# The last group of attention: denominators summed on TensorE without transfers, reciprocals on VectorE, a split projection and four stores

## The chip, the cores and the metric

The kernel runs on one core of a Trainium2 chip. The metric is the device time of one execution in microseconds (us). Engines are named as the profile names them: PE is TensorE, DVE is VectorE, ACT is ScalarE, POOL is GpSimd, SP is SyncE, which here only issues transfers.

## The reference

The whole is a block of three layers over x of 2 x 2048 rows of 512 numbers, all float32:

```python
x = x + 0.5 * ffn(layernorm(x))      # mixture of 64 experts, top 6, plus a shared one
x = x + attn(layernorm(x))
x = x + 0.5 * ffn(layernorm(x))
```

The change is in the attention, in its last microseconds:

```python
q = (x @ Wq + bq).reshape(b, s, 16, 32).transpose(0, 2, 1, 3)   # 16 query heads of 32
k = x @ Wk + bk                                                 # one key head, one value head
v = x @ Wv + bv
attn = softmax(einsum('bhsd,btd->bhst', q, k) / sqrt(32))
out = einsum('bhst,btd->bhsd', attn, v).transpose(0, 2, 1, 3).reshape(b, s, 512)
return out @ Wo + bo
```

## The kernel before

Five stages follow one another, each closed by a barrier of all engines: route and experts (first ffn), attention, route and experts again, and a final addition. Attention takes 8 chunks (CHUNKS) of 512 queries (QT). A chunk has 4 groups (GPC) of 4 heads (HG), so there are 32 groups, numbered G from 0 to 31; group 31 is head group 3 of chunk 7. Each group walks over 16 steps (STEPS) of 128 keys:

- PE `scores` (L1397) writes the transposed scores of one head and 128 keys, 128 x 512, into one of three PSUM banks of `pS`. ACT (L1346) takes the exponential into `prob[step % 4]`, a tile for four heads. PE `values` (L1435) adds the product with v to `pO`, whose four blocks of 32 partitions are the four heads.
- The softmax denominators are sums of `prob` over all keys. POOL `add_pair` (L1301) adds the tiles of two neighbouring steps, in two halves of 128 x 1024; there are 8 such pairs in a group. Pairs 0 and 1 are written to `acc`; pairs 2 to 7 go to a ring of three `pair` tiles and are added to `acc` by an accumulating transfer of 1 MB that POOL issues (L1309). When three such transfers have landed on each `acc`, PE `denominators` (L1445) sums `acc` over the partitions with a matrix of ones into `pD`. For every group but 31 this is done in steps 4 and 5 of the next group.
- ACT `copy_d` (L1357) copies `pD` to SBUF. SP `reciprocals` (L1238 to L1249) writes the four rows to DRAM, reads them back spread over 128 partitions (`d_in`), DVE takes the reciprocal of 128 x 16 numbers (L1553), SP writes them to DRAM and reads them back repeated 32 times (`d_rec`, 128 x 512).
- DVE `copy_o` (L1549) takes `pO` out of PSUM, and POOL `normalise` (L1322) multiplies it with `d_rec` into `o_n[g]`.
- PE `output` (L1419) projects a chunk: for each of four tiles of 128 queries, four products, one for each head group, into a bank of `pM`. DVE `output` (L1527) adds the result to `xo`, and SP stores the chunk in one transfer of 1 MB (L1273 for the last chunk). For chunks 0 to 6 this is done within the next chunk.
- In all groups but 31, PE also computes the row maxima of the next group between the scores (`maxima`, L1410), which DVE reduces (L1522).

After the last step of group 31 nothing of the next group is there to fill the engines: denominators, reciprocals, normalisation, projection and store of chunk 7 follow one after another. The order of every engine's work is written out by hand; semaphores are the only links. The code that differs for the last group is static (outside the loops).

## Time and profile before

| | |
|---|---|
| three timed runs | 3488.95, 3485.11, 3488.79 us, median 3488.79 |
| profiled execution, its own time | 3486.42 us |
| its span | 3484.9 us |
| busy over the span: PE, DVE, ACT, POOL | 84%, 59%, 44%, 62% |
| attention's last group, steps 0 to 15 | about 2675 to 2719 us of the span |
| from the last `values` to the next stage's first instruction | 2719.4 to 2768.0 us |

All times are microseconds from the start of the span. A matmul of float32 is two instructions in the trace, so a product of 128 x 512 counts as x2. What matters here is the second half of the last group and the 49 us behind it, in which the rows of the section below lie.

### The profile page before, as it was taken

How to read it: one execution, taken by the hardware profiler on the slowest of the kernel's cores; microseconds unless marked ns; L12 is line 12 of the kernel's file. 1: busy time of each engine (PE TensorE's matmuls, PEld its weight loads, DVE VectorE, ACT ScalarE, POOL GpSimd, SP SyncE). 2: the span in 40 equal slices, each digit the busy share in tenths (PEclk: the TensorE clock that was granted, in tenths of full speed). 3: DMA queues.
4: the chain of work that ended last, by engine and by line, in shares of the span. 5: the costliest groups of instructions: out<-in, count | busy, mean ns of one | idle time of the engine just before them, and what ended most of it. 6: DMA issues, size and time to landing. Idle time of an engine off the chain costs nothing. (4 is left out here: it accounts for less than half of the span.)

```text
span 3484.9 us, 50220 instructions
## 1 busy us (share of the span) xinstructions
PE 2920.2 (84%) x15152; PEld 1575.4 (45%) x15152; DVE 2072.8 (59%) x3981; ACT 1525.6 (44%) x2837; POOL 2170.1 (62%) x1329
## 2 busy tenths in 40 slices
PE   7967677498999998999999989999999598667650
PEld 4644444254554444444444444444444255444430
DVE  7932223464877777777787767767775188222222
ACT  3422222142566565566565655655656243222220
POOL 2148887110588777687787876876878321678760
PEclk9988888698899999999999999999999799888885
DMA  6469999754466666666666665756666542899998
GB/s 215 178 181 240 238 243 217 224 202 142 80 139 139 130 152 126 144 139 129 153 131 133 150 129 132 149 109 145 137 125 136 147 151 103 218 238 237 230 188 289
DMA packets 218402, 582.86 MB, mean 167 GB/s; under 512 B 34448, under 2 KB 35472, under 8 KB 193424
## 3 DMA queue, kind: packets, MB, share of 16 engines
q0 software_dynamic: 84992, 343.98, 48.7%
q1 hardware_dynamic: 133136, 235.53, 20.7%
q8 instruction: 135, 2.21, 0.3%
q14 instruction: 139, 1.14, 0.1%
HBM read 231.23 MB, written 155.25 MB: 111 GB/s over the span
## 5 line engine op out<-in xcount | busy, mean ns | idle before, releaser
L1522 DVE TENSOR_REDUCE attention_mx<-attention_pM 128x1 f32<-128x512 f32 x2048 | 1272.5, 684 | 354.3 <-PE attention_pM L1410 333.4
L1346 ACT ACTIVATE attention_prob<-attention_pS 128x512 f32<-128x512 f32 x2048 | 1064.2, 603 | 642.4 <-PE attention_pS L1397 621.9
L1301 POOL TENSOR_TENSOR attention_pair<-attention_prob 128x1024 f32<-128x1024 f32 x384 | 928.6, 2504 | 196.8 <-ACT attention_prob L1346 196.6
L1397 PE MATMUL attention_pS<-attention_qT,attention_kT 128*128 128x512 f32 x2048 | 867.8, 429 | 48.4 <-issue 22.0
L1410 PE MATMUL attention_pM<-attention_kT,attention_qT 96*128 96x512 f32 x2048 | 837.0, 417 | 19.3 <-DMA attention_qT<-q_parts 10.3
L1397 PEld LDWEIGHTS attention_pS<-attention_qT,attention_kT 128*128 128x128 f32 x2048 | 387.4, 191 | 541.9 <-ACT attention_prob L1346 336.2
L1435 PE MATMUL attention_pO<-attention_prob,attention_v 128*32 128x512 f32 x4096 | 541.6, 606 | 0.0
L625 POOL DMA_INDIRECT sum<-experts_res,c_table x256 | 403.8, 1577 | 117.1 <-issue 81.8
L1410 PEld LDWEIGHTS attention_pM<-attention_kT,attention_qT 96*128 96x128 f32 x2048 | 396.1, 195 | 121.6 <-DVE attention_mx L1522 53.0
L1301 POOL TENSOR_TENSOR attention_acc<-attention_prob 128x1024 f32<-128x1024 f32 x128 | 307.4, 2472 | 178.9 <-ACT attention_prob L1346 178.7
L654 PE MATMUL experts_pT<-c_ident,experts_rows 128*128 128x128 f32 x1024 | 208.7, 371 | 242.1 <-DMA experts_rows<-xn_rows,c_table 235.8
L732 DVE COPY experts_xT<-experts_pT 128x512 f32<-128x512 f32 x128 | 88.5, 692 | 534.7 <-PE experts_pT L654 532.9
L609 POOL DMA_INDIRECT experts_rows<-xn_rows,c_table x256 | 249.5, 974 | 102.3 <-issue 71.3
L654 PEld LDWEIGHTS experts_pT<-c_ident,experts_rows 128*128 128x128 f32 x1024 | 168.4, 215 | 291.9 <-DMA experts_rows<-xn_rows,c_table 261.9
L1309 POOL DMA_DIRECT2D attention_acc<-attention_pair x192 | 169.4, 882 | 128.9 <-POOL attention_pair L1301 121.7
L668 PE MATMUL experts_pU<-experts_xT,experts_wup 128*64 128x256 f32 x2048 | 236.9, 384 | 2.0 <-DVE experts_xT L732 2.0
L699 ACT ACTIVATE experts_xT<-experts_pT 128x512 f32<-128x512 f32 x128 | 76.4, 597 | 359.5 <-PE experts_pT L654 359.5
L668 PEld LDWEIGHTS experts_pU<-experts_xT,experts_wup 128*64 128x64 f32 x2048 | 142.9, 138 | 115.1 <-issue 51.4
L267 POOL TENSOR_TENSOR route_eqp<-route_eq,route_count 128x1536 f32<-128x1536 bf16 x16 | 52.5, 3279 | 212.7 <-ACT route_count L373 212.7
L1435 PEld LDWEIGHTS attention_pO<-attention_prob,attention_v 128*32 128x32 f32 x4096 | 83.7, 108 | 200.9 <-issue 127.2
L681 PE MATMUL experts_pD<-experts_wdn,experts_hid 64*128 64x512 f32 x512 | 145.6, 692 | 3.7 <-DVE experts_hid L740 2.8
L713 ACT ACTIVATE experts_res<-experts_pD,experts_rows 128x512 f32<-128x512 f32 x128 | 87.8, 687 | 111.7 <-PE experts_pD L681 93.5
(125 smaller groups left out, 2408.9 us busy)
## 6 DMA issues: line engine op xcount, KB each, us to landing
attention_acc<-attention_pair POOLq DMA_DIRECT2D x192, 1024.0 KB, 7.8
experts_wup<-in_L_ffn_w_up_dram SPq DMA_DIRECT2D x128, 256.0 KB, 4.8
attention_qT<-q_parts SPq DMA_DIRECT2D x96, 256.0 KB, 7.2
xn_rows<-route_xn SPq DMA_DIRECT2D x16, 1152.0 KB, 6.0
sum<-route_sh SPq DMA_DIRECT2D x16, 1024.0 KB, 4.4
experts_wdn<-in_L_ffn_w_down_dram SPq DMA_DIRECT2D x64, 256.0 KB, 5.0
attentionp_got<-sum SPq DMA_DIRECT2D x16, 1024.0 KB, 8.9
combine_got<-sum SPq DMA_DIRECT2D x16, 1024.0 KB, 8.2
```

The source lines that it names most:

```text
L609: pool.indirect_dma_start(rows[e % RING][:, a * HALVES + h, :], None, xn_d, bass.IndirectOffsetOnAxis(ap=k["table"][:, 2 * e + a, h:h + 1] ...
L625: pool.indirect_dma_start(sums[a], bass.IndirectOffsetOnAxis(ap=k["table"][:, 2 * e + a, h:h + 1], axis=0), res[e % 2][:, a, h, :], None, ...
L654: t = pe.transpose(pT[:, half, o:o + P], rows[e % RING][:, a * HALVES + h, c:C:CK], k["ident"][:, :])
L668: t = pe.matmul(pU[b][a * H:(a + 1) * H, v, :], wup[b][:, a, c, v * H:(v + 1) * H], xT[b][:, c, a, :], start=c == 0, stop=c == CK - 1)
L681: pe.matmul(pD[:, h, a, :], hid[b][own, h * P:(h + 1) * P], wdn[b][own, :], start=True, stop=True).then_inc(s_dn[a], 1)
L1301: pool.tensor_tensor(to[:, part], prob[2 * n % PROBS][:, part], prob[(2 * n + 1) % PROBS][:, part], ALU.add).then_inc(s_pair, 1)
L1309: pool.dma_start(acc[g % 2][n % 2][:, :], pair[(n - 2) % MOVED][:, :], accum_op=ALU.add).then_inc(s_acc[g % 2][n % 2], 16)
L1346: act.activation(prob[t % PROBS][:, h * QT:(h + 1) * QT], pS[:, at, :], ACT.Exp).then_inc(s_ex, 1)
L1397: pe.matmul(pS[:, at, :], kT[:, key:key + P], qT[g][:, h, :], start=True, stop=True).then_inc(s_sc, 1)
L1410: pe.matmul(pM[:, r % 3, :], qT[g][0:3 * DH, h, t * P:(t + 1) * P], kT[0:3 * DH, key:key + 512], start=True, stop=True).then_inc(s_mp, 1)
L1435: ins = pe.matmul(pO[h * DH:(h + 1) * DH, :], v_sb[:, batch * STEPS + t, :], prob[t % PROBS][:, h * QT:(h + 1) * QT], start=t == 0, stop=t ...
L1522: dve.tensor_reduce(mx[:, unit, part:part + 1], pM[:, r % 3, :], X, ALU.max).then_inc(s_mr, 1)
```

## The change

In group 31 alone, POOL writes its eight pair sums to eight places in `acc` and `pair` (`last_pair`) and issues no accumulating transfer. PE multiplies each pair with the matrix of ones as soon as a step of the list `LAST_SUM_STEPS` comes (pairs 0 to 5 in steps 8 to 12 and 14, pairs 6 and 7 behind the last step), all adding up in `pD`. POOL's `normalise` of group 30 is moved ahead of pair 7; that of group 31 goes away. DVE takes the reciprocal of `pD` straight from PSUM and multiplies `pO` with it, in four quarters of 128 columns. PE projects head groups 0 to 2 of each query tile ahead, and adds head group 3 when its quarter is there; the fourth tile uses a bank of `pS`. ACT's copy of `pD`, SP's ten transfers for group 31 and DVE's copy of `pO` go away. The chunk is stored in four transfers of 256 KB.

```diff
+        LAST_SUM_STEPS = (8, 9, 10, 11, 12, 14)
+        last_pair = [acc[1][0], acc[1][1], pair[0], pair[1], pair[2], acc[0][0], acc[0][1], pair[0]]
+        def last_out(t):
+            return pM[:, t, :] if t < 3 else pS[:, 0, :]
@@ SP
-                    reciprocals(CHUNKS - 1, g)
-                sp.wait_ge(s_mr, A + items_before(CHUNKS - 1, GPC - 1) + HG)
-                sp.dma_start(xo_view[CHUNKS - 1, :, :, :], xo[:, :, :]).then_inc(s_xs, 16)
+                    if g < GPC - 1:
+                        reciprocals(CHUNKS - 1, g)
+                for t in range(HG):
+                    sp.wait_ge(s_mr, A + items_before(CHUNKS - 1, GPC - 1) + (t + 1))
+                    sp.dma_start(xo_view[CHUNKS - 1, :, t, :], xo[:, t, :]).then_inc(s_xs, 16)
@@ POOL
+                        if f == 0 and last and n >= 2 + MOVED:
+                            pool.wait_ge(s_sum, A + G * 2 + (3 if n == STEPS // 2 - 1 else 0))
-                        to = acc[g % 2][n] if n < 2 else pair[(n - 2) % MOVED]
+                        to = last_pair[n] if last else acc[g % 2][n] if n < 2 else pair[(n - 2) % MOVED]
-                    if n >= 2:
+                    if n >= 2 and not last:
+                            if last and n == STEPS // 2 - 2:
+                                normalise(c, g - 1)
-                normalise(CHUNKS - 1, GPC - 1)
@@ PE
+                def last_sums(n):
+                    G = GROUPS - 1
+                    pe.wait_ge(s_pair, A + G * STEPS + 2 * (n + 1))
+                    for h in range(HG):
+                        ins = pe.matmul(pD[h * DH:(h + 1) * DH, :], k["ones32"][:, :],
+                                        last_pair[n][:, h * QT:(h + 1) * QT], start=n == 0, stop=n == STEPS // 2 - 1)
+                def last_output(t, groups):
+                    if t == 0 and 0 in groups:
+                        pe.wait_ge(s_on, A + GROUPS - 1)
+                    if GPC - 1 in groups:
+                        pe.wait_ge(s_lon, A + t + 1)
+                    for g in groups:
+                        ins = pe.matmul(last_out(t), o_n[g][:, t * P:(t + 1) * P], wo_sb[:, g, :], start=g == 0,
+                                        stop=g == GPC - 1)
+                        if last and s in LAST_SUM_STEPS:
+                            last_sums(LAST_SUM_STEPS.index(s))
+                last_sums(6)
+                first = tuple(range(GPC - 1))
+                last_output(0, first)
+                last_sums(7)
+                last_output(1, first)
+                last_output(2, first)
+                last_output(0, (GPC - 1,))
+                last_output(3, first)
+                for t in range(1, HG):
+                    last_output(t, (GPC - 1,))
@@ DVE
+                def last_quarter(t):
+                    part = slice(t * P, (t + 1) * P)
+                    dve.reciprocal(d_rec[:, part], pD[:, part]).then_inc(s_lrec, 1)
+                    dve.tensor_tensor(o_n[GPC - 1][:, part], pO[:, part], d_rec[:, part], ALU.mult).then_inc(s_lon, 1)
```

PE's instructions at the end of attention before the change, from the `values` of the last step on (four heads' products stand in one or two rows):

```order
L1435 MATMUL attention_pO<-attention_prob3,attention_v 32x512 [waits attention_ex]
L1435 MATMUL attention_pO<-attention_prob3,attention_v 32x512 x3
L1445 MATMUL attention_pD<-attention_acc10,c_ones32 32x512 [waits attention_dc,attention_acc10]
L1445 MATMUL attention_pD<-attention_acc10,c_ones32 32x512 x3
L1445 MATMUL attention_pD<-attention_acc11,c_ones32 32x512 [waits attention_acc11]
L1445 MATMUL attention_pD<-attention_acc11,c_ones32 32x512 x3
L1419 MATMUL attention_pM<-attention_wo,attention_o_n0 128x512 [waits attention_on,attention_mr]
L1419 MATMUL attention_pM<-attention_wo,attention_o_n1 128x512
L1419 MATMUL attention_pM<-attention_wo,attention_o_n2 128x512
L1419 MATMUL attention_pM<-attention_wo,attention_o_n3 128x512
```

The same place on PE after the change, to the projection of the first tile:

```order
L1455 MATMUL attention_pO<-attention_prob3,attention_v 32x512 [waits attention_ex]
L1455 MATMUL attention_pO<-attention_prob3,attention_v 32x512 x3
L1475 MATMUL attention_pD<-attention_acc01,c_ones32 32x512 [waits attention_pair]
L1475 MATMUL attention_pD<-attention_acc01,c_ones32 32x512 x3
L1488 MATMUL attention_pM<-attention_wo,attention_o_n0 128x512 [waits attention_on]
L1488 MATMUL attention_pM<-attention_wo,attention_o_n1 128x512
L1488 MATMUL attention_pM<-attention_wo,attention_o_n2 128x512
L1475 MATMUL attention_pD<-attention_pair0,c_ones32 32x512 [waits attention_pair]
L1475 MATMUL attention_pD<-attention_pair0,c_ones32 32x512 x3
```

And PE's last rows of attention after the change, from the third tile's first three head groups on:

```order
L1488 MATMUL attention_pM<-attention_wo,attention_o_n0 128x512
L1488 MATMUL attention_pM<-attention_wo,attention_o_n1 128x512
L1488 MATMUL attention_pM<-attention_wo,attention_o_n2 128x512
L1488 MATMUL attention_pM<-attention_wo,attention_o_n3 128x512 [waits attention_lon]
L1488 MATMUL attention_pS<-attention_wo,attention_o_n0 128x512 [waits attention_ex]
L1488 MATMUL attention_pS<-attention_wo,attention_o_n1 128x512
L1488 MATMUL attention_pS<-attention_wo,attention_o_n2 128x512
L1488 MATMUL attention_pM<-attention_wo,attention_o_n3 128x512 [waits attention_lon] x2
L1488 MATMUL attention_pS<-attention_wo,attention_o_n3 128x512 [waits attention_lon]
```

The sums no longer wait for a transfer (`acc10`, `acc11`) but for POOL's pair sums, nine of the twelve products of head groups 0 to 2 have no wait for group 31 ahead of them in the queue, and only four products stand behind a wait on DVE (`lon`).

POOL's last rows of attention before the change (pairs 5, 6 and 7, then the normalisations of groups 30 and 31):

```order
L1309 DMA attention_acc11<-attention_pair0 128x2048 [waits attention_pair,attention_acc11]
L1301 TENSOR_TENSOR attention_pair1<-attention_prob0,attention_prob1 128x1024 [waits attention_ex,attention_acc11]
L1301 TENSOR_TENSOR attention_pair1<-attention_prob0,attention_prob1 128x1024 [waits attention_ex]
L1309 DMA attention_acc10<-attention_pair1 128x2048 [waits attention_pair,attention_acc10]
L1301 TENSOR_TENSOR attention_pair2<-attention_prob2,attention_prob3 128x1024 [waits attention_ex,attention_acc10]
L1301 TENSOR_TENSOR attention_pair2<-attention_prob2,attention_prob3 128x1024 [waits attention_ex]
L1309 DMA attention_acc11<-attention_pair2 128x2048 [waits attention_pair,attention_acc11]
L1322 TENSOR_TENSOR attention_o_n2<-attention_o_n2,attention_d_rec 128x512 [waits attention_oc,attention_ri]
L1322 TENSOR_TENSOR attention_o_n3<-attention_o_n3,attention_d_rec 128x512 [waits attention_oc,attention_ri]
```

POOL's last rows after it:

```order
L1318 TENSOR_TENSOR attention_acc00<-attention_prob2,attention_prob3 128x1024 [waits attention_ex,attention_sum]
L1318 TENSOR_TENSOR attention_acc00<-attention_prob2,attention_prob3 128x1024 [waits attention_ex]
L1318 TENSOR_TENSOR attention_acc01<-attention_prob0,attention_prob1 128x1024 [waits attention_ex,attention_sum]
L1318 TENSOR_TENSOR attention_acc01<-attention_prob0,attention_prob1 128x1024 [waits attention_ex]
L1339 TENSOR_TENSOR attention_o_n2<-attention_o_n2,attention_d_rec 128x512 [waits attention_oc,attention_ri]
L1318 TENSOR_TENSOR attention_pair0<-attention_prob2,attention_prob3 128x1024 [waits attention_ex,attention_sum]
L1318 TENSOR_TENSOR attention_pair0<-attention_prob2,attention_prob3 128x1024 [waits attention_ex]
```

The transfers are gone from the queue, the normalisation of group 30 with its wait for `d_rec` (`ri`) now stands ahead of the last pair, and that of group 31 is no longer POOL's.

## Rows read from the trace of the kernel before

**Rows 1.** Windows of the end: length, busy us by engine, PEclk, DMA share, GB/s.
```profile
2680.00:2719.40 39.40, 35.84 (x192) 11.87 (x190) 0.25 (x1) 29.41 (x57) 35.61 (x18) 1.00 0.60 120
2719.40:2746.40 27.00, 3.87 (x16) 0.40 (x16) 0.94 (x2) 0.60 (x1) 9.31 (x7) 0.56 0.51 108
...
2746.40:2750.00 3.60, 3.52 (x4) 1.51 (x5) 0.00 (x0) 0.00 (x0) 0.00 (x0) 0.50 0.00 0
2750.00:2763.00 13.00, 12.22 (x29) 5.14 (x27) 2.75 (x4) 0.00 (x0) 0.00 (x0) 1.00 0.00 0
```

**Rows 2.** Timeline behind the last step: start, us, engine, line, idle before.
```profile
2717.26 2.10 PE L1435 MATMUL attention_pO<-attention_prob,attention_v 128*32 128x512 f32 x16
...
2733.64 1.93 PE L1445 MATMUL attention_pD<-attention_acc,c_ones 128*32 128x512 f32 x8 [4.32 <-DMA attention_acc<-attention_pair]
2735.64 0.60 ACT L1357 ACTIVATE attention_d<-attention_pD 128x512 f32<-128x512 f32 x1 [17.39 <-PE attention_pD L1445]
...
2740.19 0.34 SPq L1243 DMA_DIRECT2D d_parts<-attention_d_in  x1
2741.62 1.71 SPq L1249 DMA_DIRECT2D attention_d_rec<-d_parts  x4
2745.07 1.26 POOL L1322 TENSOR_TENSOR attention_o_n<-attention_o_n,attention_d_rec 128x512 f32<-128x512 f32 x1 [16.27 <-DMA attention_d_rec<-d_parts]
...
2746.48 15.74 PE L1419 MATMUL attention_pM<-attention_wo,attention_o_n 128*128 128x512 f32 x32 [10.91 <-POOL attention_o_n L1322]
...
2758.82 0.69 DVE L1527 TENSOR_TENSOR attention_xo<-attention_xo,attention_pM 128x512 f32<-128x512 f32 x1 [2.75 <-PE attention_pM L1419]
...
2762.26 0.69 DVE L1527 TENSOR_TENSOR attention_xo<-attention_xo,attention_pM 128x512 f32<-128x512 f32 x1 [2.75 <-PE attention_pM L1419]
2762.97 0.41 SPq L1273 DMA_DIRECT2D sum<-attention_xo  x1
2768.00 0.58 POOL L252 MEMSET route_zero<- 128x576 f32 x1 [21.67 <-POOLq L1206]
```

**Rows 3.** Timeline of ACT in the last group, steps 5 to 15.
```profile
2691.40 2.07 ACT L1346 ACTIVATE attention_prob<-attention_pS 128x512 f32<-128x512 f32 x4 [1.41 <-PE attention_pS L1397]
2694.87 2.06 ACT L1346 ACTIVATE attention_prob<-attention_pS 128x512 f32<-128x512 f32 x4 [1.40 <-PE attention_pS L1397]
2696.79 0.63 ACT L1357 ACTIVATE attention_d<-attention_pD 128x512 f32<-128x512 f32 x1
...
2710.53 2.06 ACT L1346 ACTIVATE attention_prob<-attention_pS 128x512 f32<-128x512 f32 x4 [0.55 <-PE attention_pS L1397]
2713.57 2.06 ACT L1346 ACTIVATE attention_prob<-attention_pS 128x512 f32<-128x512 f32 x4 [0.97 <-PE attention_pS L1397]
2716.18 2.06 ACT L1346 ACTIVATE attention_prob<-attention_pS 128x512 f32<-128x512 f32 x4 [0.55 <-PE attention_pS L1397]
```

**Rows 4.** Timeline of POOL, pairs 6 and 7.
```profile
2714.74 4.99 POOL L1301 TENSOR_TENSOR attention_pair<-attention_prob 128x1024 f32<-128x1024 f32 x2
...
2721.02 4.92 POOL L1301 TENSOR_TENSOR attention_pair<-attention_prob 128x1024 f32<-128x1024 f32 x2
2726.61 0.88 POOL L1309 DMA_DIRECT2D attention_acc<-attention_pair  x1 [0.67 <-POOL attention_pair L1301]
2727.23 1.57 POOL L1322 TENSOR_TENSOR attention_o_n<-attention_o_n,attention_d_rec 128x512 f32<-128x512 f32 x1
```

**Rows 5.** Timeline of SP's queue for group 30's reciprocals.
```profile
2715.27 3.94 SPq L1249 DMA_DIRECT2D attention_d_rec<-d_parts  x4
```

**Rows 6.** The two kinds of reciprocal, from the groups by line.
```profile
L1553 DVE RECIPROCAL attention_d_in<-attention_d_in 128x16 f32<-128x16 f32 x32 | 7.8, 245 | 54.1 <-DMA attention_d_in<-d_parts 54.1
L472 DVE RECIPROCAL route_wrec<-route_wsum 128x4 f32<-128x4 f32 x16 | 2.7, 170 | 0.0
```

**Rows 7.** DMA issues from 2660 to 2768: KB each, median us to landing.
```profile
sum<-attention_xo SPq DMA_DIRECT2D x1, 1024.0 KB, 4.4
attention_d_rec<-d_parts SPq DMA_DIRECT2D x12, 64.0 KB, 5.3
```

More of the change, by code:

```diff
@@ L1181, in attention @@
         s_shift = m.sem("shift")
+        s_lrec = m.sem("lrec")
+        s_lon = m.sem("lon")
         s_x = m.sem("x")
@@ L1285, in add_pair @@
                     first = g == 0 and isinstance(c, int) and c == 0
+                    last = isinstance(c, int) and c == CHUNKS - 1 and g == GPC - 1
                     for f in range(2):
@@ L1292, in add_pair @@
                             pool.sem_inc(k["pool_on"], 1)
-                        if f == 0 and n >= 2 and not (first and n < 2 + MOVED):
+                        if f == 0 and last and n >= 2 + MOVED:
+                            pool.wait_ge(s_sum, A + G * 2 + (3 if n == STEPS // 2 - 1 else 0))
+                            pool.sem_inc(k["pool_on"], 1)
+                        elif f == 0 and n >= 2 and not (first and n < 2 + MOVED):
                             old = n - MOVED if n >= 2 + MOVED else n + 6 - MOVED
@@ L1325, in body @@
                     for g in range(GPC):
+                        last = g == GPC - 1 and isinstance(c, int) and c == CHUNKS - 1
                         for n in range(STEPS // 2):
                             add_pair(c, g, n)
+                            if last and n == STEPS // 2 - 2:
+                                normalise(c, g - 1)
+                        if last:
+                            continue
                         if g > 0:
@@ L1508, in _ @@
                 chunks(body)(pe)
-                for n in range(2):
-                    denominators(CHUNKS - 1, GPC - 1, n)
-                base = items_before(CHUNKS - 1, GPC - 1)
-                for t in range(HG):
-                    output(base, t, CHUNKS - 1, t)
+                last_sums(6)
[8 more added lines that the diff above has]
+                    last_output(t, (GPC - 1,))
             @block.vector
             def _(dve):
-                begin(dve, s_mr, s_mx, s_shift, s_shd, s_rec, s_oc)
+                begin(dve, s_mr, s_mx, s_shift, s_shd, s_rec, s_oc, s_lrec, s_lon)
                 def maxima(base, r, n):
@@ L1583, in group @@
                             copy_shift(G + 1, (g + 1) % GPC, h)
-                    else:
-                        copy_o(c, g)
                 def body(c, batch):
```

26 lines of the change are left out of this document (22 added, 4 removed).

## The prediction

> **What bounds the kernel now.** I looked first at the windows of the end of attention [rows 1], because the change touches nothing else. Up to 2719.4 PE is the busy engine: 35.84 of 39.40 us, at the full granted clock (2.4 GHz). From 2719.4 to 2746.4 no engine does much: PE has 3.87 us of work in 27.0, POOL 9.31, and the clock falls to a mean of 0.56. Then PE alone works, 0.88 us an instruction while the clock is 0.50 (1.2 GHz; 3.52 us for 4) and 0.42 at 1.00 (12.22 us for 29). The reader is to see that this is a stretch of latencies, not of throughput.
>
> The timeline [rows 2] gives the links. The last `values` ends at 2719.36. POOL's pair 7 ends at 2725.94 [rows 4], its accumulating transfer is issued from 2726.61, and PE, idle for 4.32 us, can sum only at 2733.64. From ACT's copy at 2735.64 to POOL's last normalisation at 2745.07 the trip of the reciprocals through DRAM takes 9.4 us, the normalisation 1.26. PE projects from 2746.48 to 2762.22, four tiles of 4 products one after another; DVE's last addition ends at 2762.95; the store of 1 MB is issued at 2762.97 and takes a median of 4.4 us to land [rows 7]; the next stage's first instruction is at 2768.00. From 2719.36 that is 48.6 us. Whatever is taken from this chain comes off the time one for one, since a barrier follows.
>
> **The change part by part.** I rebuild the same chain with the new order, from the same rows.
>
> *Sums inside the steps.* They use PE where it is needed for the scores. Their price stands in the trace: in steps 4 and 5 of the same group PE does exactly such a sum for group 30, and ACT's exponentials there start 2694.87 - 2691.40 = 3.47 us apart, against 2716.18 - 2713.57 = 2.61 us in plain steps [rows 3]. One sum costs 0.86 us. Five of the six in the loop (steps 8 to 12) stand ahead of the last scores, so the last exponentials start 5 x 0.86 = 4.3 us later. Against this, ACT's start at 2713.57 is 3.04 us after the one before, 0.43 over the pace: there it waited for POOL to free a `prob` tile, POOL's pairs being 2721.02 - 2714.74 = 6.28 us apart with the transfer's issue between them. Without those issues a pair takes 4.99 [rows 4], less than two steps with sums (6.94), so the 0.43 goes. Last exponentials: 2716.18 + 4.3 - 0.43 = 2720.05, ending at 2722.1.
>
> *POOL.* Pair 6 needs the first two heads of step 13, whose exponentials started at 2710.53 and are delayed by four sums: 2710.53 + 3.44 + 1.04 = 2715.0. It ends at about 2720.1 (4.99). Then the normalisation of group 30, 1.57, to 2721.7, if `d_rec` is there. Pair 7's data is ready at 2721.1, so it starts at 2721.7 and ends at 2726.6 (4.92).
>
> Is `d_rec` there? Its chain starts with ACT's copy at 2696.79 [rows 3], and in the trace its last four issues end at 2715.27 + 3.94 = 2719.21 [rows 5]. That was beside POOL's accumulating transfers of 1 MB (DMA share 0.60 [rows 1]). Alone on the queues, the same chain took 9.4 us [rows 2]. In the changed kernel no such transfer is left in group 31, so I take 2696.8 + 9.4 = 2706.2, and keep as the other end 2719.21 + 5.3 (median landing of these transfers [rows 7]) = 2724.5.
>
> *PE behind the loop.* In the trace the last `values` ends 3.18 us after the last exponentials start (2719.36 - 2716.18). With sum 5 ahead of it that is 2720.05 + 3.18 + 0.86 = 2724.1. Then sum 6, 0.86, to 2725.0. Then three products of tile 0. A tile of four took 2762.26 - 2758.82 = 3.44 us at full clock, 0.86 a product: 2.6, to 2727.5. Pair 7 was ready 0.9 us before. Sum 7 to 2728.4. Six products of tiles 1 and 2: 5.15, to 2733.5. Head group 3 of tile 0, 0.86, to 2734.4; three of tile 3, 2.6, to 2737.0; the three last, 2.6, to 2739.6. PE has no wait over 1 us in all this, so I take the full clock; the 1.8 us that the four slow instructions cost before (4 x 0.46) are saved with it.
>
> *DVE.* A reciprocal of 128 x 128 doesn't occur before. Two sizes do: 128 x 4 takes 170 ns, 128 x 16 takes 245 [rows 6]. Twelve more columns cost 75 ns, 6.25 ns each, so 128 columns are 245 + 112 x 6.25 = 945 ns. Bounds: not under 0.25 (16 columns), not over 8 x 0.245 = 2.0 (eight times 16 columns). The product of a quarter is under the 0.69 us of an addition of 512 columns [rows 2]; I take 0.35. A quarter is thus 1.3 us, with bounds 0.6 and 2.7. From 2728.4 the four are done at 2729.7, 2731.0, 2732.3 and 2733.6. PE asks for the first at 2733.5 and for the other three at 2737.0, 2737.9 and 2738.7. All are hidden behind PE's products. At 2.7 a quarter they come at 2731.1, 2733.8, 2736.5 and 2739.2: 0.5 us on the path, no more. The Trainium skill (VectorE: DVE Perf Modes, on the pipeline's eight slices) says that the reciprocal is an iterative divide with a repeat count of 8; at its 0.96 GHz that would be an estimated 8.3 ns a column and 1.2 us for 128, where the two rows give 6.25 and 0.95. By either figure the sum stays as it is.
>
> *End.* The last addition is 2739.7 to 2740.4. Before, from its end to the next stage was 2768.00 - 2762.95 = 5.05 us, of which 4.4 was the landing of 1 MB. Now the last store is 256 KB, the others being on their way 0.9 us or more before. A landing of 8 KB took 1.43 us (issued 2740.19, followed at 2741.62 [rows 2]). Between 1.43 and 4.4 for 1 MB, a quarter of the difference is 0.75: 2.2 us. I take 2.2, with 1.4 and 4.4 as ends. Next stage: 2740.4 + 5.05 - 2.2 = 2743.2.
>
> The Trainium skill (DMA: Bandwidth & Descriptors, on measured bandwidth and in its rules) speaks against this part: it wants 1 MiB or more per transfer. Its fit of 2.0 us plus the bytes at 436 GB/s would make an estimated 2.6 us of 256 KB and 4.4 of 1 MB, so the last store would save 1.8 us, where the rows here give 2.2; the rule is about throughput, and only the last landing is on the path.
>
> **The sum.** 2768.0 - 2743.2 = 24.8 us less. Put otherwise: in the loop the change costs 4.7 us (2724.1 against 2719.36), and the 48.6 us behind it become 19.1. The profiled execution took 3486.42 us (its span 3484.9 and 1.5 around it): 3461.6. It lies 2.4 us below the median of the three timed runs, 3488.79, from which the same saving gives 3464.0. The four times known lie between 3485.1 and 3489.0, with 3487.6 in their middle, so I forecast 3463.
>
> **The rivals.**
> (a) *The reciprocals of group 30 come late and hold POOL.* POOL's queue has pair 7 behind the wait, and PE has sum 7 and all else. For: the other end above, 2724.5. Then the normalisation ends at 2726.1, PE's tile 0 ends at 2728.7, pair 7 at 2731.0, and sum 7 starts 3.5 us later than forecast. Against: nothing is left on the queues that would slow the chain. Saving 21.3: 3466.
> (b) *The clock falls in the new tail.* At 0.50 a product is 1.76 us and a sum 1.93 [rows 1, 2]: 16 x 0.9 + 2 x 1.07 = 16.5 us more. Saving 8.3: 3479. For: it happened in this place before. Against: PE had then been idle for several us, and now is not.
> (c) *The parts don't do what they say*: the four stores land no earlier than one (4.4 instead of 2.2), and sums cost more than 0.86 since `pO` and `pD` accumulate in turns, say 1.3 us each. With eight sums on the path, saving 24.8 - 2.2 - 8 x 0.44 = 19.1: 3468.
> (d) *Slower.* The sums make the steps so dense that the granted clock falls within the loop from step 8 on. Eight steps, each 2.61 us and most with 0.86 more, double at 1.2 GHz: 8 x 2.61 + 6 x 0.86 = 26 us more, and (b)'s 16.5 on top, 42.5 against 24.8 saved: 18 us slower, 3505. It decides once the tail and about three of the eight steps run at half clock (16.5 + 2.6 x 3.25 = 24.8). Against: the clock was 1.00 throughout the last group with PE busy 35.84 of 39.40 us.
> (e) *No difference.* The next stage would have to wait for something that the tail doesn't move. Nothing in the rows does: in the 5 us ahead of the next stage's first instruction no engine works and only the store is in flight.
>
> **How the numbers follow.** Forecast 0.80; (a) 0.06; (c) 0.05; (b) 0.05; (d) 0.02; (e) 0.02. Within 0.2%, 7 us, is about what a measurement of this kernel can't tell from no change; of (a), (b) and (c) all lie beyond it. Faster 0.96, same 0.02, slower 0.02. For the range: the forecast's own bounds are the landing (0.8 less, 2.2 more), `d_rec` (3.5 more), DVE (0.5 more) and the spread of the runs, 4 us from the lowest to the highest. That is 3459 to 3470; it holds (a) and (c), and leaves out (b), (d) and (e).
>
> **What would show it.** In the profile of the changed kernel: ACT's exponentials 3.5 us apart in steps 10 to 14 and the last ones at about 2720; no accumulating transfer after the last of group 30; POOL's normalisation of group 30 directly behind pair 6 with no wait for `d_rec`; the granted clock 1.00 to 2740; PE without a wait over 1 us from the last `values` to its last product at 2739.6; DVE's reciprocals of 128 columns near 0.95 us each, and PE's head group 3 not waiting for them; the next stage's first instruction at about 2743. The forecast is wrong if the clock falls, if POOL waits for `d_rec`, if a sum costs much over 0.86 us, or if the later stages change their length, which nothing here foresees.

## The result and the profile after

The changed kernel takes 3462.43 us (median of 4 runs, 3461.33 to 3466.65) against 3487.65 for the kernel before (3485.11 to 3488.95 in 4 runs). The ratio is 0.9928, with a 95% interval from 0.9913 to 0.9942: 25.2 us faster. The profiled execution took 3461.33 us, its span is 3459.2.

All of the stretch that was rebuilt in the prediction can be read from a few lines. The windows of the new end, in the columns of [rows 1] (length; busy us of PE, PEld, which is PE's weight load, DVE, ACT and POOL; granted clock, DMA share, GB/s):

```profile
2679.00:2719.00 40.00, 37.10 (x213) 12.61 (x213) 0.25 (x1) 27.34 (x53) 32.37 (x15) 1.00 0.12 27
2719.00:2739.00 20.00, 19.64 (x75) 7.20 (x73) 6.89 (x12) 2.07 (x4) 5.93 (x3) 1.00 0.05 19
2739.00:2742.30 3.30, 0.00 (x0) 0.00 (x0) 0.58 (x1) 0.00 (x0) 0.02 (x1) 1.00 0.57 209
```

Where PE had worked 3.87 of 27.0 us, it now works 19.64 of 20.0, at the full granted clock, and transfers hardly take place (DMA share 0.12 and 0.05 against 0.60 and 0.51). PE's timeline behind the loop, with the last two steps' `values` (`pO`) and sums 5, 6 and 7 (`pD`):

```profile
2719.66 0.50 PE L1417 MATMUL attention_pS<-attention_qT,attention_kT 128*128 128x512 f32 x1 [0.21 <-ACT attention_prob L1367]
2720.09 1.07 PE L1455 MATMUL attention_pO<-attention_prob,attention_v 128*32 128x512 f32 x8
2720.97 1.04 PE L1475 MATMUL attention_pD<-attention_acc,c_ones 128*32 128x512 f32 x8
2721.83 1.04 PE L1455 MATMUL attention_pO<-attention_prob,attention_v 128*32 128x512 f32 x8
2722.69 1.04 PE L1475 MATMUL attention_pD<-attention_acc,c_ones 128*32 128x512 f32 x8
2723.66 2.84 PE L1488 MATMUL attention_pM<-attention_wo,attention_o_n 128*128 128x512 f32 x6
2726.43 1.07 PE L1475 MATMUL attention_pD<-attention_pair,c_ones 128*32 128x512 f32 x8
2727.43 6.28 PE L1488 MATMUL attention_pM<-attention_wo,attention_o_n 128*128 128x512 f32 x14
2733.54 2.74 PE L1488 MATMUL attention_pS<-attention_wo,attention_o_n 128*128 128x512 f32 x6
2736.11 1.88 PE L1488 MATMUL attention_pM<-attention_wo,attention_o_n 128*128 128x512 f32 x4
2737.83 1.02 PE L1488 MATMUL attention_pS<-attention_wo,attention_o_n 128*128 128x512 f32 x2
```

No row behind the first has a wait in brackets: the chain is PE's own work from 2719.66 to 2738.85. The other engines on the timeline, ACT's last exponentials, POOL's pair 6, the moved normalisation and pair 7, DVE's first quarter and last addition, and the next stage's start:

```profile
2716.39 2.06 ACT L1367 ACTIVATE attention_prob<-attention_pS 128x512 f32<-128x512 f32 x4 [1.40 <-PE attention_pS L1417]
2719.01 2.07 ACT L1367 ACTIVATE attention_prob<-attention_pS 128x512 f32<-128x512 f32 x4 [0.55 <-PE attention_pS L1417]
...
2714.28 4.71 POOL L1318 TENSOR_TENSOR attention_acc<-attention_prob 128x1024 f32<-128x1024 f32 x2 [2.22 <-ACT attention_prob L1367]
2718.96 1.29 POOL L1339 TENSOR_TENSOR attention_o_n<-attention_o_n,attention_d_rec 128x512 f32<-128x512 f32 x1
2720.65 4.68 POOL L1318 TENSOR_TENSOR attention_pair<-attention_prob 128x1024 f32<-128x1024 f32 x2 [0.41 <-ACT attention_prob L1367]
...
2727.57 0.96 DVE L1655 RECIPROCAL attention_d_rec<-attention_pD 128x128 f32<-128x128 f32 x1 [27.27 <-PE attention_pD L1475]
2728.56 0.29 DVE L1659 TENSOR_TENSOR attention_o_n<-attention_pO,attention_d_rec 128x128 f32<-128x128 f32 x1
...
2738.89 0.69 DVE L1665 TENSOR_TENSOR attention_xo<-attention_xo,attention_pS 128x512 f32<-128x512 f32 x1 [0.17 <-PE attention_pS L1488]
...
2742.28 0.58 POOL L252 MEMSET route_zero<- 128x576 f32 x1 [16.94 <-POOLq L1216]
```

For comparing runs I use one stretch of the trace: from the start of ACT's exponentials of step 2 in group 31 to the next stage's first instruction. It is 2768.00 - 2680.09 = 87.9 us before and 2742.28 - 2679.03 = 63.25 us after, 24.7 less. In these two executions what follows it is equally long (3484.9 - 2768.0 = 3459.2 - 2742.3 = 716.9). The last 1.06 us of difference between the two spans lie ahead of the stretch, in code that the change doesn't touch.

That the rest is equal is partly chance. Over the 14 profiled executions of this study (one for each kernel, and a second one of the changed kernel) the stretch started anywhere from 2678.9 to 2685.8, and what follows it, whose code is the same in all of them, took from 707.4 to 720.9 us: 710.0 in the second execution of the changed kernel. So differences of a few us are read from the stretch and not from the medians. Each stretch is that of one execution.

### The profile page after: what moved, and what is told of

Its sections match the earlier page's. It is cut to its first block and busy times, and to the rows that moved or that the text cites. A ratio compares the mean times of both kernels' runs of the same rounds, so it can differ in the third digit from the quotient of the medians.

```text
span 3459.2 us, 50292 instructions
## 1 busy us (share of the span) xinstructions
PE 2922.8 (84%) x15200; PEld 1577.6 (46%) x15200; DVE 2074.2 (60%) x3987; ACT 1524.8 (44%) x2836; POOL 2164.4 (63%) x1322
## 5 line engine op out<-in xcount | busy, mean ns | idle before, releaser
L1318 POOL TENSOR_TENSOR attention_pair<-attention_prob 128x1024 f32<-128x1024 f32 x380 | 919.2, 2506 | 199.0 <-ACT attention_prob L1367 198.9
L1318 POOL TENSOR_TENSOR attention_acc<-attention_prob 128x1024 f32<-128x1024 f32 x132 | 317.3, 2479 | 182.3 <-ACT attention_prob L1367 182.0
L713 ACT ACTIVATE experts_res<-experts_pD,experts_rows 128x512 f32<-128x512 f32 x128 | 87.9, 687 | 110.4 <-PE experts_pD L681 80.8
```

The source lines that it names most:

```text
L1318: pool.tensor_tensor(to[:, part], prob[2 * n % PROBS][:, part], prob[(2 * n + 1) % PROBS][:, part], ALU.add).then_inc(s_pair, 1)
```

## Experiments

All variants start from the changed kernel unless said otherwise. Measured is the stretch defined above, from the profiled execution. The ratio is that of the medians of all runs, against the kernel before on the same chip, with its 95% interval. `...` in an edit stands for lines left out.

**The changed kernel once more.** No edit.

> The changed kernel once more, to see how well a stretch of the trace repeats. The stretch that all runs here are read by goes from the start of ACT's exponentials of step 2 in group 31 to the next stage's first instruction. It is 87.9 us in the kernel before (2680.09 to 2768.00) and 63.3 in the changed one (2679.03 to 2742.28). Theory (the end is a chain on PE, set by constant durations): 63.3, within 0.2. Rival (part of the 24.7 us is chance): it moves by a microsecond or more. The time: 0.7% under the kernel before.

Measured: 63.18 us (2678.88 to 2742.06). Ratio 0.9925 (0.9912 to 0.9939). The stretch repeats within 0.1 us in these two executions, so it can tell parts of a microsecond.

**The sums by accumulating transfers again.**

```diff
-                        to = last_pair[n] if last else acc[g % 2][n] if n < 2 else pair[(n - 2) % MOVED]
+                        to = acc[g % 2][n] if n < 2 else pair[(n - 2) % MOVED]
...
-                    if n >= 2 and not last:
+                    if n >= 2:
...
-                            if last and n == STEPS // 2 - 2:
-                                normalise(c, g - 1)
...
-                        if last and s in LAST_SUM_STEPS:
-                            last_sums(LAST_SUM_STEPS.index(s))
...
-                last_sums(6)
+                denominators(CHUNKS - 1, GPC - 1, 0)
...
                 last_output(0, first)
-                last_sums(7)
+                denominators(CHUNKS - 1, GPC - 1, 1)
```

> The changed kernel with the old way of the sums: group 31's pairs 2 to 7 are again added to acc by six accumulating transfers, POOL normalises group 30 after pair 7, PE sums twice behind the loop. The reciprocals on DVE, the split projection and the four stores stay. Theory: the loop gets its 4.7 us back, but group 30's normalisation ends only 48.7 us into the stretch and the second sum waits for the transfer at 53.6; then 13 products (11.2 us), the addition (0.8) and the last landing (2.7) follow: 69 to 73 us, with the upper end if the clock falls while PE waits. So 6 to 9 us of the 24.7 are the sums' place. Rival (the sums on PE gain nothing, since they cost in the loop what they save): 63 to 65 us.

Measured: 69.59 us (2683.57 to 2753.16), ratio 0.9944 (0.9929 to 0.9959). PE's timeline:

```profile
2720.72 2.10 PE L1447 MATMUL attention_pO<-attention_prob,attention_v 128*32 128x512 f32 x16
2730.83 1.93 PE L1457 MATMUL attention_pD<-attention_acc,c_ones 128*32 128x512 f32 x8 [8.01 <-DMA attention_acc<-attention_pair]
2732.69 4.67 PE L1480 MATMUL attention_pM<-attention_wo,attention_o_n 128*128 128x512 f32 x6
2737.30 1.06 PE L1457 MATMUL attention_pD<-attention_acc,c_ones 128*32 128x512 f32 x8
```

PE stands idle for 8.01 us before the transfers into the first `acc` have landed, and then runs slowly (granted clock 0.50 from 2730.8 to 2736): the first three products take 4.67 us instead of 2.84. In the loop one step again takes 2717.03 - 2713.99 = 3.04 us instead of 2.61: the 0.43 us that the prediction puts down to POOL, which frees a `prob` tile late when it has a transfer to issue. The sums' new place is worth 6.3 us, though it costs time within the loop. The rival that it gains nothing is refuted.

**The reciprocals through DRAM again.**

```diff
-                    if g < GPC - 1:
-                        reciprocals(CHUNKS - 1, g)
+                    reciprocals(CHUNKS - 1, g)
...
                 chunks(body)(pool)
+                normalise(CHUNKS - 1, GPC - 1)
...
                 chunks(body)(act)
+                act.wait_ge(s_sum, A + (GROUPS - 1) * 2 + STEPS // 2)
+                copy_d(GROUPS - 1)
...
-                        pe.wait_ge(s_lon, A + t + 1)
+                        pe.wait_ge(s_on, A + GROUPS)
```

> The changed kernel with the old way of the reciprocals of group 31: ACT copies pD, SP takes it through DRAM, DVE copies pO, POOL normalises. Sums on PE, split projection and four stores stay. Theory: sum 7 ends 48.4 us into the stretch, the trip takes 9.4 and the normalisation 1.3, so head group 3 can start at 59.2; PE has nine products (7.7 us) to hide it behind and then waits 3 us: 66.2 us if the clock holds, up to 70 if the last four products run at 1.2 GHz. Rival (the products ahead hide the trip): 63.3.

Measured: 71.07 us (2685.77 to 2756.84), ratio 0.9952 (0.9937 to 0.9968). That is 7.8 us over the changed kernel, and 1 us over the top of what I expected. The timeline from the last sum on:

```profile
2734.14 5.42 PE L1490 MATMUL attention_pM<-attention_wo,attention_o_n 128*128 128x512 f32 x12
2734.28 0.60 ACT L1378 ACTIVATE attention_d<-attention_pD 128x512 f32<-128x512 f32 x1 [6.49 <-PE attention_pD L1477]
...
2743.80 1.26 POOL L1338 TENSOR_TENSOR attention_o_n<-attention_o_n,attention_d_rec 128x512 f32<-128x512 f32 x1 [11.75 <-DMA attention_d_rec<-d_parts]
...
2745.12 2.07 PE L1490 MATMUL attention_pM<-attention_wo,attention_o_n 128*128 128x512 f32 x2 [5.56 <-POOL attention_o_n L1338]
...
2746.99 3.85 PE L1490 MATMUL attention_pS<-attention_wo,attention_o_n 128*128 128x512 f32 x6
```

The trip took 9.5 us as before. I had counted nine products to hide it behind, but the queue holds only six ahead of the waiting one: `last_output(0, (3,))` stands before the three products of tile 3. PE waited 5.56 us with work behind the wait, and about 2.1 us of slower clock came on top: its last 14 instructions take 8.29 us, where the same 14 take 6.17 in the changed kernel (granted clock 0.50 from 2745.1 to 2748.6). This also shows that rival (b), the slower clock, was a real danger of this tail: it came back behind PE's wait of 5.56 us here and of 8.01 us in the run before.

**The projection whole, at the end.**

```diff
-                first = tuple(range(GPC - 1))
-                last_output(0, first)
                 last_sums(7)
-                last_output(1, first)
-                last_output(2, first)
-                last_output(0, (GPC - 1,))
-                last_output(3, first)
-                for t in range(1, HG):
-                    last_output(t, (GPC - 1,))
+                for t in range(HG):
+                    last_output(t, tuple(range(GPC)))
```

> The changed kernel without the split: PE does sums 6 and 7 and then the four tiles with all four head groups each, behind DVE's quarters. Theory: PE waits for pair 7 (1.8 us) and for the first quarter (1.3 us), nothing else changes: 63.3 + 2.5 = 65.8 us. Rival (the split is worth nothing, PE has the same 16 products): 63.3. Second rival (the gaps let the clock fall): above 70.

Measured: 66.24 us (2682.60 to 2748.84), ratio 0.9934 (0.9919 to 0.9949). In the trace PE waits 1.65 us for pair 7 and 1.50 for DVE's first quarter, and the clock holds (1.00 from 2720 to 2746):

```profile
2728.89 1.07 PE L1475 MATMUL attention_pD<-attention_pair,c_ones 128*32 128x512 f32 x8 [1.65 <-POOL attention_pair L1318]
2731.45 10.54 PE L1488 MATMUL attention_pM<-attention_wo,attention_o_n 128*128 128x512 f32 x24 [1.50 <-DVE attention_o_n L1653]
```

The split is worth 3.0 us, which is the two waits that it fills, and not the 10 us that its twelve products take.

**One store.**

```diff
-                for t in range(HG):
-                    sp.wait_ge(s_mr, A + items_before(CHUNKS - 1, GPC - 1) + (t + 1))
-                    sp.dma_start(xo_view[CHUNKS - 1, :, t, :], xo[:, t, :]).then_inc(s_xs, 16)
...
+                sp.wait_ge(s_mr, A + items_before(CHUNKS - 1, GPC - 1) + HG)
+                sp.dma_start(xo_view[CHUNKS - 1, :, :, :], xo[:, :, :]).then_inc(s_xs, 16)
```

> The changed kernel with one store of 1 MB in place of four of 256 KB. Theory: the landing is 4.4 instead of 2.2 us, so the stretch is 65.4 instead of 63.3 us. By the 2.0 us plus bytes at 436 GB/s of the Trainium skill (DMA: Bandwidth & Descriptors) an estimated 65.1. Rival (a landing costs the same whatever its size here): 63.3.

Measured: 65.59 us (2678.89 to 2744.48), ratio 0.9937 (0.9921 to 0.9952): 2.3 us for a last landing of 1 MB instead of 256 KB. The DMA view gives 4.4 us for the one store here, and in the changed kernel a median of 2.0 us for the four:

```profile
sum<-attention_xo SPq DMA_DIRECT2D x4, 256.0 KB, 2.0
attention_d_rec<-d_parts SPq DMA_DIRECT2D x4, 64.0 KB, 2.0
```

**The six sums behind the loop.**

```diff
-        LAST_SUM_STEPS = (8, 9, 10, 11, 12, 14)
+        LAST_SUM_STEPS = ()
...
-                last_sums(6)
+                for n in range(7):
+                    last_sums(n)
```

> The changed kernel with pairs 0 to 5 summed behind the last step instead of within steps 8 to 14. Theory (PE's own work is the chain, a sum costs 0.86 us in either place): 63.3 us within 0.3, while the last exponentials start 4.3 us earlier. Rival (in the loop a sum also breaks the rhythm of scores and exponentials, so it is dearer there): 1 to 3 us less. Second rival (POOL's pair 7, which then waits for PE's third sum, is late): more.

Measured: 63.44 us (2682.25 to 2745.69), ratio 0.9932 (0.9917 to 0.9947). The last exponentials start 4.3 us earlier in the stretch (2717.94 - 2682.25 = 35.7 us into it instead of 40.0), and the end is the same. A sum costs 0.86 us of PE in either place: steps 8 to 14 hid none of it. POOL's pair 7 now had to wait 4.17 us for PE's third sum, as the second rival feared, but it ended at 2728.88, still ahead of sum 7 at 2729.84.

**DVE adds the pairs, PE sums twice.** This and the next try to beat the changed kernel.

```diff
-        LAST_SUM_STEPS = (8, 9, 10, 11, 12, 14)
+        LAST_SUM_STEPS = ()
...
+                for n in range(1, STEPS // 2 - 1):
+                    dve.wait_ge(s_pair, A + (GROUPS - 1) * STEPS + 2 * (n + 1))
+                    dve.wait_ge(s_ladd, A + n - 1)
+                    dve.tensor_tensor(last_pair[0][:, :], last_pair[0][:, :], last_pair[n][:, :], ALU.add
+                                      ).then_inc(s_ladd, 1)
...
```

> The changed kernel with DVE, which is idle in group 31, adding pairs 1 to 6 to pair 0, and PE summing twice instead of eight times, both times behind the loop. Theory (PE's work is the chain): six sums of 0.86 us go, 63.3 - 5.2 = 58.1 us, with DVE's adds of 128 x 2048 at about 2.3 us each hidden. Rival (DVE and POOL hinder one another in SBUF): POOL's halves grow over 2.4 us, pair 7 comes late, and the stretch is 60 us or more.

Measured: 70.21 us (2683.79 to 2754.00), ratio 0.9946 (0.9932 to 0.996). It is 7 us slower than the changed kernel instead of 5 faster. POOL's pairs and DVE's first adds in the timeline:

```profile
2699.92 4.71 POOL L1322 TENSOR_TENSOR attention_pair<-attention_prob 128x1024 f32<-128x1024 f32 x2 [2.22 <-ACT attention_prob L1371]
2705.14 8.67 POOL L1322 TENSOR_TENSOR attention_pair<-attention_prob 128x1024 f32<-128x1024 f32 x2 [0.51 <-ACT attention_prob L1371]
2713.78 15.47 POOL L1322 TENSOR_TENSOR attention_acc<-attention_prob 128x1024 f32<-128x1024 f32 x4
...
2704.99 2.23 DVE L1657 TENSOR_TENSOR attention_acc<-attention_acc 128x2048 f32<-128x2048 f32 x1
2707.32 13.04 DVE L1657 TENSOR_TENSOR attention_acc<-attention_acc,attention_pair 128x2048 f32<-128x2048 f32 x3
```

The moment that DVE adds, a pair takes POOL 8.67 us instead of 4.71, and DVE's own additions go from 2.23 to 4.3. Pairs 4 to 7 come late, and ACT and PE wait for them. Part of the loss is again the clock: behind PE's waits of 3.73 and 3.05 us it is granted 0.59 (2723.3 to 2727.5) and 0.68 (2732.6 to 2737.9). By these figures that is an estimated 3.4 of the 7 us.

**The same with `values` one place earlier.**

```diff
                         for h in range(HG if s < STEPS - 1 else 0):
+                            if last and h == HG - 1:
+                                values(G, s, batch)
...
                             scores(G, g, s + 1, h, batch)
...
```

> The kernel of the run before with PE's values of a step placed between the third and the fourth head's scores in group 31, where PE waits for the first exponential. Theory: PE waited there 0.2 us and the exponentials 0.55 us a step; a step falls from 2.61 us to POOL's pace of about 2.4, over 13 steps 2.7 us: 55.4 us. Rival (POOL's adds or ACT set the step already): 58.

Measured: 70.8 us (2683.9 to 2754.74), ratio 0.9952 (0.9939 to 0.9966), 0.6 us slower than the run before. The edit begins with step 0, so ACT's row at 2683.40 holds the last head of step 1 and three heads of step 2, whose first exponential starts at 2683.9. The expectation was badly reasoned whatever DVE did: plain steps stayed at 2.61 us (ACT's rows start at 2683.40, 2686.01, 2688.63). Four scores and one block follow one another in a circle, and moving the block by one place only renames the heads.

**DVE busy with additions that nobody needs.** Six additions wo + wo into a tile of its own, with the sums on PE as in the changed kernel.

```diff
+                for n in range(6):
+                    dve.wait_ge(s_idle, A + n)
+                    dve.tensor_tensor(idle[:, :, :], wo_sb[:, :, :], wo_sb[:, :, :], ALU.add).then_inc(s_idle, 1)
...
```

> The changed kernel with six additions on DVE from about 20 us into the stretch that nobody waits for: wo + wo, 128 x 2048, into a tile of its own. It adds work that the reference doesn't have. Theory (DVE and POOL hinder one another when both read and write SBUF, whatever the data): POOL's halves go from 2.36 to about 4.35 us while DVE adds, DVE's adds from 2.23 to about 4.4, and the stretch grows by some 4 to 6 us to 67 to 69. Rival (POOL was slow in the run with DVE's adds since they shared tiles or waits): POOL's halves stay at 2.36 and the stretch at 63.3.

Measured, in its one execution: 69.26 us (2683.70 to 2752.96), 6.0 us more than the changed kernel. From the groups by line between 2704 and 2729:

```profile
L1653 DVE TENSOR_TENSOR attention_idle<-attention_wo 128x2048 f32<-128x2048 f32 x6 | 23.9, 3992 | 0.2
L1320 POOL TENSOR_TENSOR attention_acc<-attention_prob 128x1024 f32<-128x1024 f32 x4 | 17.5, 4416 | 0.0
```

No tile, no semaphore and no wait are shared, and still POOL's halves take 4.42 us instead of 2.36 and DVE's additions 3.99 instead of 2.23. So additions of both engines at the same time are enough to slow both. The Trainium skill (SBUF — State Buffer, Who interferes with whom) has this rule: a DVE `tensor_tensor` with both inputs in SBUF contends with GpSimd's reads, and the loser is blocked for the whole instruction. The trace agrees in the main: if each waits for the other's instruction and then does its own, both take 2.36 + 2.23 = 4.59 us, and POOL's take 4.42, DVE's 3.99 on average. DVE's work in the changed kernel has at most one operand in SBUF or comes behind POOL's last pair, and POOL's pairs stay at 4.71 us there.

The stretch grew by PE's waits and by the clock, which here fell behind a wait of only 1.77 us:

```profile
2723.25 0.75 PE L1419 MATMUL attention_pS<-attention_qT,attention_kT 128*128 128x512 f32 x1 [1.77 <-ACT attention_prob L1369]
2723.93 1.93 PE L1457 MATMUL attention_pO<-attention_prob,attention_v 128*32 128x512 f32 x8
```

From 2723.2 to 2727.6 it is granted 0.61, an estimated 1.7 of the 6.0 us.

**`values` and sums in halves.**

```diff
                             scores(G, g, s + 1, h, batch)
+                            if last and h % 2:
+                                half = (h - 1, h)
+                                values(G, s, batch, half)
...
+                                if s in LAST_SUM_STEPS:
+                                    last_sums(LAST_SUM_STEPS.index(s), half)
...
```

> The changed kernel, with PE's values of a step (and the sums) in group 31 cut in two: heads 0 and 1 stand behind the scores of head 1, heads 2 and 3 behind those of head 3. Moving the whole block, as in the run before, only turned the same cycle of four scores and one block; this changes it, since no block is longer than 0.5 us. Theory (the steps are paced by the ring of three score banks, which ACT empties while PE spends 1.0 us on values): plain steps go from 2.61 us to POOL's 2.36, steps with a sum from 3.47 to PE's own 2.8, together 5 to 6.5 us: a stretch of 57 to 58 us instead of 63.3. Rival (PE's work as such fills the steps, or the halves lose the overlap of the four heads): 62 us or more.

Measured: 79.6 us (2680.13 to 2759.74), ratio 0.9967 (0.9957 to 0.9978), 16 us slower than the changed kernel. Steps 0 and 1, ahead of the stretch, are halved too and take 0.7 us more. PE's timeline has the reason:

```profile
2680.26 1.05 PE L1455 MATMUL attention_pO<-attention_prob,attention_v 128*32 128x512 f32 x4
2681.24 0.73 PE L1417 MATMUL attention_pS<-attention_qT,attention_kT 128*128 128x512 f32 x2
2681.91 1.05 PE L1455 MATMUL attention_pO<-attention_prob,attention_v 128*32 128x512 f32 x4
```

Two heads (x4) take 1.05 us, as four heads (x8) take 1.07 in the changed kernel. The four heads write to four different blocks of 32 partitions, and the second pair of heads costs 0.02 us beside the first; halving the block saves nothing and doubles the number of blocks.

**Six products moved into the steps of that kernel.**

```diff
+        EARLY_OUT = (1, 2, 3, 6, 7, 13)
...
+                                if h == HG - 1 and s in EARLY_OUT:
+                                    n = EARLY_OUT.index(s)
+                                    last_output(n % 3, (n // 3,))
...
```

> The kernel of the run before, and six of the twelve products of head groups 0 to 2 (tiles 0 to 2 of groups 0 and 1, whose o_n is ready) moved into the plain steps 1, 2, 3, 6, 7 and 13. Theory: with POOL at 2.36 us a step PE has some 0.4 us to spare there, so each product costs about 0.45 in the loop and saves 0.86 behind it: 2.4 us less than the run before. Rival (PE has nothing to spare): the same as the run before.

Measured: 79.6 us (2683.26 to 2762.89), ratio 0.9972 (0.9962 to 0.9982), as the rival had it. ACT's pairs of exponentials, 1.65 us apart in plain halves, are 2.51 apart where a product stands: with blocks in halves PE is full, and a product costs its 0.86 wherever it is.

**Whole blocks, kept apart.** From the changed kernel: the sum of a step stands between the scores of heads 1 and 2, and six products take that place in plain steps. The order behind the loop changes too: tile 3's first three products now follow sum 7, and all four products of head group 3 stand at the very end.

```diff
+        EARLY_OUT = (1, 2, 3, 6, 7, 13)
...
                             scores(G, g, s + 1, h, batch)
+                            if last and h == 1:
...
+                                if s in LAST_SUM_STEPS:
+                                    last_sums(LAST_SUM_STEPS.index(s))
+                                if s in EARLY_OUT:
+                                    n = EARLY_OUT.index(s)
+                                    last_output(n % 3, (n // 3,))
...
-                last_output(0, first)
+                for t in range(HG - 1):
+                    last_output(t, (GPC - 2,))
                 last_sums(7)
-                last_output(1, first)
-                last_output(2, first)
-                last_output(0, (GPC - 1,))
                 last_output(3, first)
-                for t in range(1, HG):
+                for t in range(HG):
                     last_output(t, (GPC - 1,))
```

> The changed kernel with whole blocks, but not next to one another: in group 31 the sum of a step stands between the scores of heads 1 and 2 and values behind those of head 3; the six products of tiles 0 to 2 of head groups 0 and 1 stand in the place of the sum in steps 1, 2, 3, 6, 7 and 13. Theory (PE waits 0.22 us a step for ACT, and 0.6 us of ACT's idle time a step can take in a block if it isn't adjacent to values): a step with a sum falls from 3.47 to about 3.2 us, a plain step with a product grows from 2.61 to about 3.0 while 0.86 goes behind the loop, so 7 x 0.25 + 6 x 0.46 = 4.5 us: a stretch of 58 to 60. Rival (in the steps PE's work adds up wherever it stands): a product costs its 0.86 in the step and nothing is won, 63 us.

Measured: 59.90 us (2682.59 to 2742.49), 3.35 us less than the changed kernel, in the range of the theory. Ratio 0.9916 (0.9902 to 0.9929), median 3458.49 us; this interval overlaps that of the changed kernel, so the medians alone don't prove the gain. ACT's rows in steps with a product and in steps with a sum:

```profile
2683.92 1.09 ACT L1368 ACTIVATE attention_prob<-attention_pS 128x512 f32<-128x512 f32 x2 [0.24 <-PE attention_pS L1418]
2685.57 1.08 ACT L1368 ACTIVATE attention_prob<-attention_pS 128x512 f32<-128x512 f32 x2 [0.56 <-PE attention_pS L1418]
2686.89 1.09 ACT L1368 ACTIVATE attention_prob<-attention_pS 128x512 f32<-128x512 f32 x2 [0.24 <-PE attention_pS L1418]
...
2704.13 1.08 ACT L1368 ACTIVATE attention_prob<-attention_pS 128x512 f32<-128x512 f32 x2 [0.57 <-PE attention_pS L1418]
2705.79 1.08 ACT L1368 ACTIVATE attention_prob<-attention_pS 128x512 f32<-128x512 f32 x2 [0.58 <-PE attention_pS L1418]
2707.45 1.08 ACT L1368 ACTIVATE attention_prob<-attention_pS 128x512 f32<-128x512 f32 x2 [0.57 <-PE attention_pS L1418]
```

A step with a product takes 2686.89 - 2683.92 = 2.97 us, 0.36 over a plain one, for 0.86 of work; a step with a sum takes 2707.45 - 2704.13 = 3.32 instead of 3.47. So six products gain 6 x 0.50 = 3.0 us and the sums 0.15 a step, about 1.0 for seven. Together they make 4.0, and PE's last product does end 4.0 us earlier in the stretch (2738.41 - 2682.59 = 55.8 us into it instead of 59.8). The stretch shows 3.35, and the 0.65 between lies in DVE's queue and the stores:

```profile
2737.04 1.87 DVE L1670 TENSOR_TENSOR attention_xo<-attention_xo,attention_pM 128x512 f32<-128x512 f32 x3
2738.83 0.68 DVE L1670 TENSOR_TENSOR attention_xo<-attention_xo,attention_pS 128x512 f32<-128x512 f32 x1
```

DVE's quarters end only at 2737.12, so the four additions follow one another and the last one ends 1.10 us behind PE instead of 0.73. The four stores are then issued within 2.12 us instead of 5.48, and the next stage starts 2.62 us behind the end of the last issue instead of 2.35.

## Why the prediction was right

The stretch was forecast to lose 24.8 us and lost 24.7. Point by point, with 1.06 us taken off the forecast's instants because the stretch began that much earlier:

- *Sums inside the steps.* The price of 0.86 us, taken from steps 4 and 5 [rows 3], held in every step: ACT's idle time before a step is 1.40 us there against 0.55. The last exponentials were forecast for 2719.0 and started at 2719.01. The 0.43 us put down to POOL went away with the transfers' issues, and it came back in the run that has them.
- *POOL.* Pair 6 took 4.71 and the normalisation 1.29 instead of 4.99 and 1.57, and pair 7 started at 2720.65 (forecast 2720.6). That this agrees to 0.1 us is luck: the two shorter durations were made up for by a pair 6 that started 0.3 us later than forecast and by 0.41 us of waiting ahead of pair 7, which the profile puts down to ACT. `d_rec` was no obstacle: the normalisation has no wait for it, and the four 64 KB transfers landed in a median of 2.0 us instead of 5.3 [rows 7]. Rival (a) did not occur.
- *PE behind the loop.* No wait, full clock, last product at 2738.85 against a forecast of 2738.5. The text ahead of the prediction says that nine of the twelve products of head groups 0 to 2 have no wait for group 31 ahead of them. That is so only of waits for DVE: the first three stand behind sum 6 and the next six behind sum 7, which wait for POOL's pairs 6 and 7, and only these six stand between sum 7 and the first wait for DVE. Rival (b) did not occur; in the two runs whose PE waited 5.56 and 8.01 us, the half clock came back, and behind some shorter waits in the runs with DVE's additions too.
- *Rivals (c) and (d).* A sum cost 0.86 us and the last store of 256 KB landed in 2.0, so (c) did not occur. The clock was 1.00 in the loop and behind it, so neither did (d).
- *DVE.* A reciprocal of 128 x 128 takes 0.96 us where two small sizes [rows 6] had given 0.945; a quarter takes 1.19 us. They are hidden, and with PE's tile 0 waiting for nothing, the split projection is what hides them: without it 1.5 us of them show.
- *End.* 256 KB landed in 2.0 us, forecast 2.2, and one store of 1 MB costs 2.3 us more, forecast 2.2. The Trainium skill's rule of 1 MiB or more (DMA: Bandwidth & Descriptors, rules for kernel authors) would have kept the store whole; by its fit, which that page gives for transfers issued by GpSimd while these are SP's, the difference was an estimated 1.8 us.
- *The sum.* The next stage starts at 2742.28, forecast 2742.1. The median of 3462.43 lies 0.6 us under the forecast of 3463. That closeness is luck: the four runs spread over 5.3 us, and what lies outside the stretch moved by more than that between executions. What the study confirms is the 24.7 us of the stretch.

Taken back one at a time, the parts are worth 6.3 (sums), 7.8 (reciprocals), 3.0 (split) and 2.3 us (stores), 19.5 together. The missing 5.2 belong to no single part: they appear only when several are undone, for a wait that one part leaves open is partly filled by another's work. That is argued from the four runs; no run undoes two parts at once.

Where I erred was in the expectations behind the prediction: the queue order in the DRAM variant (six products ahead of the wait, not nine), DVE as a free helper, the circle of scores and `values`, and the price of half a block.

## What to carry to other kernels

A tail in which every engine waits for another can be rebuilt from the rows of its own trace to a few tenths of a microsecond, if every moved instruction is given its place in its queue; then ask what has become the chain, here PE's own work. Filling is worth no more than the waits that it fills (3.0 us for twelve products). A sum costs less when it stands apart from the other long block of its step (0.71 us) than next to it (0.86), and a product of 0.86 us costs 0.36 there; why the product is so much cheaper than the sum, and what it would cost next to `values`, no run shows. Before idle DVE is given additions in SBUF, look at whether POOL is adding there at the same time. And a wait that seems short can cost more than its length, since the clock may fall behind it (here behind one of 1.77 us).

## What was not expected of the hardware

- DVE additions with both operands in SBUF and POOL additions slow each other to 3.99 and 4.42 us from 2.23 and 2.36, with no data in common.
- Products whose outputs are 32 partitions wide, in different blocks: two heads take 1.05 us and four take 1.07.
- The length of PE's wait alone doesn't tell whether the clock falls behind it. It was granted 1.00 behind waits of 1.50 and 1.65 us (the whole projection) and of 2.52 (DVE's adds), and 0.61 behind one of 1.77 (DVE's additions that nobody needs). What decides it stays open.
- The start of the stretch moved by up to 7 us between kernels whose code ahead of it is the same but for steps 0 and 1 of group 31 in three of them, while the stretch itself repeated to 0.1 us. Whether that is chance or goes with the program stays open: the two executions of the changed kernel agreed within 0.15 us there, but differed by 6.9 us (716.9 and 710.0) behind the stretch.
